# Early loads, one mask block, shared statistics, and the places of sums, reciprocals and an x reload in a four-layer attention kernel

## What is computed

```python
x = x + tanh(g_xattn[l]) * xattn_l(layernorm(x), ctx, ...)
x = x + tanh(g_ffn[l]) * ffn_l(layernorm(x), ...)
```

```python
q, k, v = heads(xn @ Wq.T + bq), heads(ctx @ Wk.T + bk), heads(ctx @ Wv.T + bv)
out = (softmax(q @ k.T / sqrt(32)) @ v) @ Wo.T + bo
# L1: scores clipped to +-50, masked keys at -50, and the result through a LayerNorm
# L2: xn and Wq, the heads and Wp pass through an int8 quantise-and-back; L3: plain
```

## Time and profile before

| | us |
|---|---|
| median of 3 runs (lowest to highest) | 3059.93 (3059.43 to 3064.61) |
| the profiled execution | 3059.54 |
| its span | 3057.8 |
| TensorE busy in it | 2632.1 (86%) |
| VectorE busy | 1753.8 (57%) |
| ScalarE busy | 1196.7 (39%) |
| GpSimd busy | 930.9 (30%) |

### The profile page before, as it was taken

The page is one execution under the profiler, slowest core; times in us unless marked ns, Lnnn a source line. Parts: engine busy times, 40 slices in busy tenths (PEclk is TensorE's granted clock), DMA queues, the critical chain, the costliest instruction groups (busy, mean ns, idle before and its releaser), DMA issues. The chain is left out here.

```text
span 3057.8 us, 36158 instructions
## 1 busy us (share of the span) xinstructions
PE 2632.1 (86%) x11447; PEld 1671.9 (55%) x11447; DVE 1753.8 (57%) x3263; ACT 1196.7 (39%) x2550; POOL 930.9 (30%) x434
## 2 busy tenths in 40 slices
PE   7998799788887679999959998738699998699898
PEld 3555487655434456656546553426476653477555
DVE  2444576467765989989377664512277773444221
ACT  0222222267743688788014555111125553222111
POOL 0222000066732110010015775033318982322122
PEclk9998899899988889999979999869899999799999
DMA  9663113665403410100063421074465430212722
GB/s 278 223 241 139 55 62 124 182 166 142 111 1 114 165 56 28 46 37 28 14 170 107 132 68 29 1 288 110 106 183 172 121 102 1 84 41 71 262 56 47
DMA packets 137548, 333.52 MB, mean 109 GB/s; under 512 B 18608, under 2 KB 21681, under 8 KB 133041
## 3 DMA queue, kind: packets, MB, share of 16 engines
q1 hardware_dynamic: 110192, 262.71, 27.7%
q0 software_dynamic: 12864, 29.06, 4.1%
q10 hardware_dynamic: 14336, 39.85, 3.9%
HBM read 237.24 MB, written 97.72 MB: 110 GB/s over the span
## 5 line engine op out<-in xcount | busy, mean ns | idle before, releaser
L1982 POOL TENSOR_TENSOR L_attn_total<-L_attn_total,L_attn_probs 128x2048 f32<-128x2048 f32 x103 | 471.8, 4581 | 31.6 <-ACT L_attn_probs L1910 22.1
L2016 DVE TENSOR_REDUCE L_attn_row_max<-L_attn_rows_ps 128x1 f32<-128x512 f32 x512 | 338.9, 684 | 149.6 <-PE L_attn_rows_ps L1776 145.5
L1910 ACT ACTIVATE L_attn_probs<-L_attn_s_ps 128x512 f32<-128x512 f32 x512 | 288.0, 601 | 269.1 <-PE L_attn_s_ps L1797 264.2
L521 PE MATMUL L_ffn_hidden<-L_ffn_x_high,L_ffn_up_high 128*128 128x512 f32 x688 | 295.9, 430 | 73.2 <-DVE L_ffn_routes L432 25.8
L1797 PE MATMUL L_attn_s_ps<-L_attn_q_stack,L_attn_k_stack 98*128 98x512 f32 (+1 forms) x768 | 311.7, 432 | 21.1 <-ACT L_attn_probs L1910 20.7
L398 ACT ACTIVATE L_ffn_sums<-sims 128x128 f32<-128x128 f32 x1024 | 314.5, 389 | 29.0 <-DVE L_ffn_routes L418 22.3
L521 PE MATMUL L_ffn_hidden<-L_ffn_x_low,L_ffn_up_high 128*128 128x512 f32 x688 | 272.8, 397 | 0.0
L1776 PE MATMUL L_attn_rows_ps<-L_attn_k_stack,L_attn_q_stack 96*128 96x512 f32 x512 | 223.1, 439 | 23.0 <-DVE L_attn_row_max L2016 17.1
L542 PE MATMUL L_ffn_y<-L_ffn_down_in,L_ffn_h 128*128 128x512 f32 x512 | 230.8, 596 | 1.9 <-DVE L_ffn_h L649 1.9
L1797 PEld LDWEIGHTS L_attn_s_ps<-L_attn_q_stack,L_attn_k_stack 98*128 98x128 f32 (+1 forms) x768 | 145.7, 194 | 158.1 <-ACT L_attn_probs L1910 73.3
L1910 ACT ACTIVATE L_attn_probs<-L_attn_s_ps,keep_mask 128x512 f32<-128x512 f32 x256 | 183.8, 783 | 82.8 <-DVE L_attn_s_ps L2028 82.4
(11 more groups left out here) (310 smaller groups left out, 4526.2 us busy)
## 6 DMA issues: line engine op xcount, KB each, us to landing
L_attn_k_stack<-k_parts SPq DMA_DIRECT2D x144, 256.0 KB, 4.8
L_attn_q_stack<-q_parts SPq DMA_DIRECT2D x72, 256.0 KB, 6.0
k_parts<-L_attn_stage SPq DMA_DIRECT2D x32, 512.0 KB, 2.8
L_attn_abs_in<-in_L_ffn_w SPq DMA_DIRECT2D x12, 1024.0 KB, 10.8
L_attn_kv_parts<-L_attn_part ACTq DMA_DIRECT2D x12, 1024.0 KB, 4.8
L_attn_ctx<-ctx_parts SPq DMA_DIRECT2D x24, 512.0 KB, 9.3
L_attn_wv<-L_attn_kv_parts SPq DMA_DIRECT2D x24, 512.0 KB, 7.1
q_parts<-L_attn_stage SPq DMA_DIRECT2D x24, 512.0 KB, 3.6
```

The source lines that it names most:

```text
L521: last = nc.tensor.matmul(hidden_ps[0:m, b, side, :], w[:, i, e0:e0 + m], x_parts[xp][:, i, h * HALF:(h + 1) * HALF], start=(q == 0), stop ...
L1910: nc.scalar.activation(probs[:, g % P_SLOTS, h, :], s_ps[:, v % S_SLOTS, :], ACT.Exp, **kinds).then_inc(exp_done, 1)
L1982: nc.gpsimd.tensor_tensor(total[:], first, probs[:, g % P_SLOTS], ALU.add).then_inc(added, 1)
L2016: nc.vector.tensor_reduce(row_max[:, hq, i:i + 1], rows_ps[:, r % R_SLOTS, :], AX_X, ALU.max, negate=True).then_inc(max_done, 1)
```

## The change

- L0_attn: SyncE loads Wo and bo into the tiles `wv` and `bv` at the end of `linear_attention_block`; `output_block` gets them as `weights` and starts without a load.
- L1_attn: `key_mask_block` is gone; the mask's DMA is the first that SyncE issues in the attention's own block, and its three VectorE operations stand ahead of the opening. The exponentials wait for them.
- L1, L2 and L3_attn: the biases (`load_biases`) are issued ahead of Wq. The standard deviations are now an item S0 of the opening.
- `ffn_block` sets `tile_stats.taken` for the sublayer behind it, so L2_attn takes no statistics.
- L2_attn: another order of the opening; `SUMS_AT` 2 instead of 7; reciprocals of 64 columns, two each in units 3 and 4 and four in unit 10, instead of 128 columns in units 8 to 11.
- L2_ffn and L3_attn: the reload of x from `x_sums` and the statistics move from the end of `routed_block` into L3_attn's block. SyncE issues the eight tiles behind the biases and ahead of Wq. The opening has another order, with S0 behind V02.

```diff
@@ ffn_block
+            env.tile_stats.taken = final
@@ routed_block
-                if not last:
-                    for t in range(TILES):
-                        sp.dma_start(env.x[:, t, :], sums[t * P:(t + 1) * P, :]).then_inc(back[t], 16)
...
-                if not last:
-                    for t in range(TILES):
-                        dve.wait_ge(back[t], 16)
-                        env.tile_stats.take(env, dve, t)
-                    env.tile_stats.finish(dve)
@@ streamed_attention_block
-    SUMS_AT = 7 if less_max_rows else PV_AT
-    INVERT_AT = {u: part for part, u in enumerate((8, 9, 10, 11) if less_max_rows else (4, 6, 7, 8, 9, 10, 11, 12))}
-    INVERTED = SEQ // len(INVERT_AT)
+    SUMS_AT = 7 if less_max_rows and not made else PV_AT
+    invert_units = (3, 3, 4, 4, 10, 10, 10, 10) if made else (8, 9, 10, 11) if less_max_rows else (4, 6, 7, 8, 9, 10, 11, 12)
+    INVERT_PARTS = len(invert_units)
+    INVERT_AT = {u: [part for part, v in enumerate(invert_units) if v == u] for u in invert_units}
+    INVERTED = SEQ // INVERT_PARTS
...
-        order = ("N0 X0 X1 N2 W0 W1 X2 X3 N4 Q00 V00 V01 X4 X5 W2 W3 N6 Q01 V02 V03 X6 X7 Q02 Q03 Q10 Q11 T0 Q12 Q13")
+        order = ("W0 W1 N0 N2 X0 X1 X2 X3 N4 Q00 W2 Q01 W3 V00 Q02 V01 N6 Q03 X4 X5 V02 X6 X7 V03 Q10 Q11 T0 Q12 Q13")
...
         order = ("N0 N1 K00 N2 N3 X0 X1 K01 N4 N5 X2 X3 W0 W1 V00 N6 N7 X4 X5 Q00 W2 W3 V01 X6 X7 Q01 K10 K11 "
                  "V02 V03 Q02 Q03 Q10 Q11 T0 Q12 Q13")
+    if x_sums is None:
+        order = "S0 " + order
+    else:
+        order = ("K00 K01 V00 V01 V02 S0 N0 N1 V03 X0 X1 W0 W1 N2 N3 X2 X3 Q00 N4 N5 W2 W3 Q01 X4 X5 N6 N7 K10 Q02 X6 X7 K11 "
+                 "Q03 Q10 Q11 T0 Q12 Q13")
...
+                if not less_max_rows:
+                    sp.dma_start(mask_raw[:], io["mask"]).then_inc(mask_loaded, 16)
+                parts.load_biases(env, sp)
+                if x_sums is not None:
+                    for t in range(TILES):
+                        sp.dma_start(env.x[:, t, :], x_sums[t * P:(t + 1) * P, :]).then_inc(x_back[t], 16)
                 parts.first_loads(env, sp)
...
+                def statistics():
+                    if not taken_before:
+                        for t in range(TILES):
+                            if x_sums is not None:
+                                dve.wait_ge(x_back[t], 16)
+                            nc.vector.bn_stats(stats[:, t, :], env.x[:, t, :]).then_inc(stats_done, 1)
+                        for t in range(TILES):
+                            dve.wait_ge(stats_done, t + 1)
+                            nc.vector.bn_aggr(meanvar[:, t, :], stats[:, t, :]).then_inc(var_done, 1)
+                    dve.wait_ge(sd_done, 1)
+                    nc.vector.reciprocal(rstd[:], sd[:]).then_inc(rstd_done, 1)
+                    dve.wait_ge(rstd_done, 1)
@@ linear_attention_block
+                sp.wait_ge(v_done, CT)
+                sp.dma_start(wv[:], wo_dram).then_inc(env.wo_loaded, 16)
+                sp.dma_start(bv[:], io["bo"].partition_broadcast(P)).then_inc(env.wo_loaded, 16)
```

More of the change, by code:

```diff
@@ L917, in _, with routed_block @@
                 dve.sem_inc(slots.placed, 1)
-def routed_block(env, name, slots, weights, load_weights, E, sums, last, ahead=None):
+def routed_block(env, name, slots, weights, load_weights, E, sums, ahead=None):
     nc = env.nc
@@ L934, in routed_block @@
     kept, summed, weighed = env.sem("kept"), env.sem("summed"), env.sem("weighed")
-    back = [env.sem(f"back{n}") for n in range(TILES)]
     weight_step = env.sem("weight_step")
@@ L1582, in streamed_attention_block @@
     env.wo_loaded = env.sem("wo_loaded")
+    x_back = [env.sem(f"x_back{t}") for t in range(TILES)] if x_sums is not None else []
     with ExitStack() as local:
@@ L1848, in _ @@
                         turn(0)
-                    elif item[0] not in "WN":
+                    elif item[0] not in "WNS":
                         for c in range(DC):
@@ L1919, in take, with deviations @@
                     nc.scalar.copy(heads, o_ps).then_inc(taken, 1)
-                act.wait_ge(parts.biases_loaded, 48)
-                if not taken_before:
-                    act.wait_ge(var_done, TILES)
-                nc.scalar.activation(sd[:], meanvar[:, :, 1], ACT.Sqrt, bias=env.eps_ln[:]).then_inc(sd_done, 1)
+                def deviations():
+                    if not taken_before:
+                        act.wait_ge(var_done, TILES)
+                    nc.scalar.activation(sd[:], meanvar[:, :, 1], ACT.Sqrt, bias=env.eps_ln[:]).then_inc(sd_done, 1)
                 act.wait_ge(parts.biases_loaded, 48)
                 for item in OPENING:
-                    if item[0] in "KQ":
+                    if item[0] == "S":
+                        deviations()
+                    elif item[0] in "KQ":
                         high_part(item)
@@ L1936, in _ @@
                         high_turn(0)
+                if not less_max_rows:
+                    act.wait_ge(mask_step, 3)
                 for n in range(SETS):
@@ L2107, in _ @@
                         if u in INVERT_AT and n:
-                            invert(n - 1, INVERT_AT[u])
+                            for part in INVERT_AT[u]:
+                                invert(n - 1, part)
                         if less_max_rows and u == TURN_AT and n + 1 < SETS:
                             low_turn(n + 1)
-                for part in range(len(INVERT_AT)):
+                for part in range(INVERT_PARTS):
                     invert(SETS - 1, part)
@@ L2503, in quantise_rows, with output_block @@
     each(lambda r: nc.vector.tensor_scalar(dst[:, r, :], tmp[:, r, :], -MAGIC, s[:, r:r + 1], ALU.add, ALU.mult))
-def output_block(env, name, heads_out, gate, wo_dram, quantised=False, after_norm=False, feature_major=False, early=None):
+def output_block(env, name, heads_out, gate, wo_dram, quantised=False, after_norm=False, feature_major=False, early=None, weights=None):
     nc, io = env.nc, env.io
@@ L2521, in sb @@
             return local.enter_context(nc.sbuf_tensor(f"{name}_{n}", shape, dt))
-        if early:
+        if weights:
+            wo, bo = weights
+        elif early:
             wo, out_rows = env.out_weights[:, 0], env.out_weights[:, 1]
@@ L2758, in x_hat, with expert_layer @@
                 yield
-        def expert_layer(name, gate, shared, normalise, sums, last=False, ahead=None):
+        def expert_layer(name, gate, shared, normalise, sums, ahead=None):
             with sublayer() as local:
```

75 lines of the change are left out of this document (30 added, 45 removed).

## The result

| | median us | runs | ratio to before (95%) |
|---|---|---|---|
| before | 3059.93 | 3056.79 to 3064.61 | |
| changed | 3087.61 | 3081.82 to 3097.24 | 1.0092 (1.0072 to 1.0111) |

A forecast was written before the change was run, and what follows sets the result against it. Idle stretches at four sublayer starts, plus TensorE's waits for row maxima and GpSimd's tight totals in L2's sets, were taken as bounds; -5.4 - 5.5 - 7 + 6 + 5 = -6.9 gave 3053.0 us beside the median, range 3039 to 3064.

The forecast's parts named there:

- Part A: L0's output product: weights loaded a block early let TensorE's first turn start sooner; -5.4 us, between -4.5 and -6.5.
- Part B: L1's opening: no separate mask block and biases ahead of Wq shorten the waits; -5.5 us, between -7.2 and -2.5.
- Part C1: L2's opening: no repeated statistics, earlier biases and a new order bring Q00 forward; -7 us, between -10 and -3.
- my charge of 2 to 3: L2's opening: 2 to 3 us charged for GpSimd's W subtractions and the memset of k_stack lying under N0.
- the 4.1 of my sum: L2's opening: with bv ahead of Wq, the standard deviations at about 1541.2 and the first pair 3.2 us earlier.
- C2: L2's sets: moving the sums and reciprocals costs time; +6 us, between -2 and +11.
- +1 for each of sets 1 to 5: L2's sets: VectorE, held at the first reciprocal until unit 4 ends, lengthens each set by 1 us; +5 together.
- the row of unit 14: L2's sets: VectorE's work up to unit 12's maximum, which frees this row's slot, takes 12.1 us against 10.9 before.
- these can go or multiply: L2's sets: three sets had a dip to half clock, about 1.5 us each, which could vanish or multiply.
- The rival on GpSimd's totals: L2's sets: delayed exponentials make each set wait at the new sum; C2 +11, kernel 3061, chance 0.18.
- D: L3's opening: the hidden 9.8 us of reload and statistics are more than spent again; +5 us, between -3 and +9.
- my +5 holds 1: L3, first row to first score: same work plus two turns (1.0 us) and half clock costing 0 to 2.4.

The follow-up runs named there:

- e7: Changed kernel with L3's start as before the change and L2's first value product's chunks moved from units 0, 1, 3, 4 to 3, 4, 5, 6; 3061.36 us.
- e11: Changed kernel with L3's start as before the change, and the edits of e7 and e3 together in L2's sets; 3046.14 us.
- e3: Changed kernel with five GpSimd additions a set instead of six in L2_attn, TensorE taking that key tile directly in the sum; 3076.82 us.
- e1: Changed kernel with L2's sums back in unit 7 and reciprocals back to four of 128 columns in units 8 to 11; 3066.05 us.
- e5: Changed kernel with L2's sets as before, x's reload issued in L2_ffn's block but awaited only in L3_attn, statistics behind K00; 3054.12 us.
- e9: As e5, but with the statistics ahead of K00 in L3's opening; 3048.31 us.

## Why the prediction was wrong, point by point

**Right.** Part A: -5.4 forecast, -5.4 measured. Part B: -5.5 forecast, -7.0 measured at the first score, inside its bounds; but bv alone took 4.3 us where I had estimated 3, so the first turn still waits, and the late table load, which the forecast did not see, takes 1.3 back. Part C1: -7 forecast, -4.1 measured. Q00 came 4.3 nearer to the block's start where I had 6.5. By the Trainium skill's rule (GPSIMD Engine Reference, "SBUF interfaces") it would have been 4, and two more forms of VectorE's work were slowed under GpSimd's (1.89 for 0.88, 1.64 for 0.69). But that 4 is met by luck: the first two pairs took 13.0 us where I had counted 10.4 undisturbed, 2.6 more and inside my charge of 2 to 3. The other 2.2 come from bv, for which the first pair waits: it starts 6.3 us into the block and not the 4.1 of my sum.

**Wrong: C2, +6 forecast, +24.6 measured.** The step that says "+1 for each of sets 1 to 5" had one mechanism right: VectorE stands at the first reciprocal until unit 4's chunk is done. In set 1, where nobody waits for a total, that comes to about 36.8 us at full clock against 35.9, the +1 forecast. The stalls fall at the rows of units 6 to 8, though, and not at the row of unit 14 by which I had measured the distance: VectorE catches up under the products with values in unit 10. In sets 2 to 5 it is about +1.4, of which 1.1 is the wait for the total, a term that the +1 had put at nothing, so that the near agreement there is luck.

What failed is above all the step after it, "these can go or multiply": I let the stretches at the lower clock average to nothing. Over the eight sets there are 47.8 us at 1.2 GHz instead of 20.5. Half of the difference, 13.7, is what that costs at most; the other 10.9 or so are waits, 7.7 in sets 1 to 5 (forecast 5) and 3.2 in the last two (forecast 1). The stretches came where the stalls are; e7 and e11, without them, have none in the full sets. They also lengthen GpSimd's circle, which waits for exponentials meanwhile. The rival on GpSimd's totals was true in kind, but priced at +11 and given 0.18. The last two sets took 10.1 more in all: the sums wait 2.2 and 4.9 for the total, and the scores behind the second run at half clock. Five additions instead of six take all of that back (e3).

**Wrong: D, +5 forecast, +15.5 measured.** Each gap was where it was said to be (4.42 and 7.28). Three terms were mis-sized. The block starts 5.0 us after the scatter has landed, not 1.4, since closing a block with GpSimd's scatters took 3.8 that the reload had covered: +3.6. From the block's start to the first row it is 51.0 instead of 48, mainly by Q00 at half clock (5.5 us from its start to its copy, where its products took 3.0 before): +3. From the first row to the first score it is 40.2 instead of 35.6, where my +5 holds 1: +3.6, at a clock of 0.90 instead of 1.00. The row on K00 behind its long gap had said so, and I had put it at the end of the range.

The range ended at 3064 because it took one bad case at a time; C2 and D were both over their ends, by 14 and 6.5.

## What to carry to other kernels

When work moves, ask what an engine in order will stand on there: the reciprocals moved "into slack" waited for a counter that a later product had to advance, and filler products moved ahead of a load left nothing to cover it. A sum taken earlier shortens nothing if what it sums is a loop of another engine: count that engine's time from sum to sum first. And where stalls of half a microsecond to one repeat in each pass, do not price them at their length alone: here the lower clock cost about as much again, and the same stalls cost nothing in some passes. A new wait ahead of an engine's work may also hold back what needed no wait, as the load of ScalarE's tables came late here.

## What the runs showed of the hardware

- TensorE's clock fell to 1.2 GHz, for 3.4 us in set 1 and 6.8 in sets 2 to 5 of the changed kernel, around stalls of 0.90, 0.67 and 0.2 to 0.6 us and although the engine was busy 37.0 of 40.7 us; the full sets without them (e7, e11) stayed at 2.4 GHz. The Trainium skill (TensorE: Matmul & The Clock Gate, Part 1) says that the low state is the default and that activity releases it. The work behind the long gaps agrees (K00 of L1: 5.08 us for 12 products behind 7.21 idle, where the next 12 took 2.98); why an engine so busy falls back, no run here shows.
- A block in which GpSimd had issued scatters closed 4.2 us after the last had landed (2208.94 to 2213.1). 3.82 of them are one instruction of GpSimd's sequencer that ends its part; it takes the same 3.82 in the kernel before and in e1, e5 and e9.
- A 0.25 MB load of one vector to all partitions took 4.3 us from issue to landing in L1 and 4.8 in L2, with nothing large ahead of it, where the 1 MB of Wq behind it took 6.5 and 7.5.
- The load of ScalarE's tables ahead of the first exponential took 1.28 us in L1, L2 and L3. In L2 and L3 it starts 0.67 us after the first score, in L1 with the wait ahead of it 2.43 us after.
